# Reordering the passage from cross-attention to a quantised FFN in a one-core Trainium2 kernel

## The chip, the cores and the metric

The kernel runs on one core of one Trainium2 chip. The metric is the device time of one execution in microseconds (us). The engines are TensorE (PE in the profile, PEld for its weight loads), VectorE (DVE), ScalarE (ACT), GpSimd (POOL) and SyncE (SP), which issues most DMAs.

## The reference

x is 64 x 64 rows of 128, the context 64 x 64 rows of 256, all fp32. The first half is masked cross-attention with 8 heads of 16 and a residual, the second a feed-forward block whose three products take inputs quantised to FP4 in blocks of 16:

```python
src = (ctx @ W_src.T + b_src) * mask          # keys, values
q   = (layernorm(x) @ W_tgt.T + b_tgt) * mask
attn = softmax(where(mask == 0, -inf, q k / 4))
x = x + concat(layernorm(x), attn @ v) @ W_out.T + b_out
def fp4_quant_dequant(x):                     # blocks of 16
    scale = max(max(abs(block)) / 6, 1e-12)
    q = grid[searchsorted(mid, abs(x / scale))] * sign(x) * scale
xq = fp4_quant_dequant(layernorm(x))
h = silu(xq @ wq_gate.T) * (xq @ wq_up.T)     # 352 wide
out = x + fp4_quant_dequant(h) @ wq_down.T
```

## The kernel before, in words

The 4096 rows are 32 tiles of 128, in NG = 8 groups of 4 tiles (0 to 7). Every engine has its own program, written out by hand; semaphores are the only tie between them, and each engine works strictly in its written order. That order is what the change edits.

**Attention.** `attn_step(k)` runs for k = 0 to 8. In one step each engine works on several groups: key, query and value projections of group k, scores and softmax of k-1, attention product, out-projection and layer norm of k-2 and k-3, and quantisation of the FFN's input of k-3 and k-4. On TensorE a step goes scores (L954), attend (L988), spread_reciprocals (L1002), transposes of the normalised x, keys (L1017), two minus_max products, queries (L1025), two more minus_max, then `prob_transpose(g2, 0)` (L982), half of the values (`v_project`, L1030), `prob_transpose` 1 and 2, the other half, the last transposes and out_project (L1039). The values need the masked q (VectorE, `q_masked`, L694), since both use the PSUM bank w0. ScalarE does exponentials (L508), copies of the transposed probabilities (`probT_evac`, L516) and of keys and values. The context comes in four buffers cT, filled on SyncE's queue (L202).

**Quantising a group's FFN input** is a chain over three engines: VectorE adds the residual (`x2_add`, L729) and takes statistics (`stats2`, L690); POOL makes the scale (`rstd2_of`, L267) and the normalised rows (`xn2_of`, L274); VectorE takes block maxima (`block_max`, L735); POOL the scales (`scales2_of`, L286); VectorE their reciprocals (`block_reciprocal`, L742); POOL y (`y_of`, L306); ScalarE its magnitude (`y2_abs`, L521); VectorE rounds in two operations (`s3_round`, L747, L750 and L754); POOL multiplies back (`xq_of`, L313). The weights go the same way once; POOL's last product over all of them is L375, in step 3.

**FFN.** 16 units of two tiles. For tile m TensorE forms gate and up (`gate_up`, L1078; three PSUM banks in turn), ScalarE the silu (L537), VectorE the product (`h_product`, L838). For each unit VectorE takes maxima and reciprocals (L847, L854), ScalarE scales them (`h_inverse`, L617), POOL multiplies (`y_unit`, L386; its scales `h_scales`, L395), ScalarE takes the magnitude (`h_abs`, L598), VectorE rounds (`h_round`, L859, L864 and L869), POOL multiplies back (`hq_unit`, L401). Seven tiles later TensorE transposes h (L1096), ScalarE copies it, and TensorE multiplies with w_down (L1109). The quantisation of groups 5, 6 and 7 is written in between the units of these loops, at tiles `m` and units `u` given by numbers such as

```python
if m == 8:
    y2_abs(NG - 2)      # ScalarE, L646: group 6
if m == 9:
    s3_round(NG - 2)    # VectorE, L934
if u == 2:
    y_of(NG - 2)        # POOL, L454
```

## Time and profile before

| | |
|---|---|
| median of 3 runs | 204.89 us (204.83 to 205.24) |
| the profiled execution | 205.46 us |
| its span, first to last instruction | 203.2 us |
| busy: TensorE, VectorE, POOL, ScalarE | 185.8, 174.8, 141.2, 132.1 us |
| granted TensorE clock, mean | 0.995 |
| attention steps 0 to 7, with the start of scores in each from step 1 | 12.8, 25.3, 38.7, 51.2, 65.7, 78.5, 91.4, 103.9 us |
| first gate product, last store | about 113.4, the span's end |

The span is the time axis of all views; start times count from its beginning. A timeline row gives start, length, engine, line, output and input, and in brackets the idle time of that engine ahead of it with what ended it. A row with x4 stands for four instructions from the first start to the last end. Lengths of TensorE rows reach into the next row, since matmuls are pipelined: what one costs is the distance to the next start.

### The profile page before, as it was taken

The page shows a single profiled execution, that of the slowest core. Times are in us where ns is not written, and L with a number is a line of the kernel's source. Part 1 is how long each engine was busy: PE and PEld are TensorE (multiplying, and loading weights), DVE is VectorE, ACT ScalarE, POOL GpSimd, SP SyncE. Part 2 cuts the span into 40 slices and gives each one's busy share as a digit, 9 for nine tenths or more (in the row PEclk, how much of TensorE's full clock was granted, in tenths as well). Part 3 has the DMA queues.
Part 4 walks back from the last instruction along what each step waited for, and adds up shares of the span by engine and source line. Part 5 has one row for each costly group of instructions (what it writes and reads, how often), then busy time and mean ns, then how long its engine had stood idle before and what let it go on. Part 6 is the DMA issues. An engine that isn't in the chain of part 4 may idle for free.

```text
span 203.2 us, 5834 instructions
## 1 busy us (share of the span) xinstructions
PE 185.8 (91%) x2105; PEld 142.6 (70%) x2105; DVE 174.8 (86%) x383; ACT 132.1 (65%) x280; POOL 141.2 (70%) x206
## 2 busy tenths in 40 slices
PE   5889989999889999999998999689999998999881
PEld 5564866859649788596785775467878676877780
DVE  6558989988998988969868888999999999999861
ACT  2066997959778699696868735485566564656740
POOL 6353691678898685954919577797999966868870
PEclk9999999999999999999999999999999999999997
DMA  5799970401200000000000000000101100110013
GB/s 199 236 239 345 353 250 7 155 5 31 75 3 2 3 3 5 0 0 3 5 3 0 3 2 0 0 5 0 53 0 55 43 9 0 55 50 5 0 59 99
DMA packets 13698, 11.99 MB, mean 59 GB/s; under 512 B 790, under 2 KB 10590, under 8 KB 13670
## 3 DMA queue, kind: packets, MB, share of 16 engines
q1 hardware_dynamic: 13086, 11.23, 18.0%
q10 hardware_dynamic: 584, 0.39, 0.6%
q8 instruction: 17, 0.28, 0.5%
q14 instruction: 11, 0.09, 0.2%
HBM read 9.52 MB, written 2.10 MB: 57 GB/s over the span
## 4 chain that ended last, share of the span: by engine, by line
PE 50%; POOL 18%; issue 12%; DVE 8%; DMA 4%; ACT 4%; SPq 1%; POOLq 0%; ACTq 0%; DVEq 0%
PE bank L1034 7%; PE bank L1125 5%; PE bank L1022 5%; POOL wq_y L391 5%; DMA x_all<-in_x 4%; POOL xn L282 3%; POOL hq L406 3%; PE bank L1093 3%; PE bank L1090 3%; PE bank L985 3%; PE bank L1105 3%; PE bank L1028 3%; PE bank L997 3%; PE bank L971 2%; PE bank L1043 2%
## 5 line engine op out<-in xcount | busy, mean ns | idle before, releaser
L1125 PE MATMUL bank<-wdT,hT 128*128 128x128 f32 x186 | 26.4, 278 | 1.8 <-issue 0.8
L1090 PE MATMUL bank<-guT,xqT 128*128 128x352 f32 x64 | 24.6, 465 | 2.2 <-DVE hh L843 2.2
L1125 PEld LDWEIGHTS bank<-wdT,hT 128*128 128x128 f32 x186 | 23.2, 191 | 3.1 <-issue 1.9
L1093 PE MATMUL bank<-guT,xqT 128*128 128x352 f32 x64 | 24.2, 460 | 0.0
L406 POOL TENSOR_TENSOR hq<-wq_u,sch 128x704 f32<-128x704 f32 x15 | 21.2, 1411 | 3.6 <-DVE wq_u L869 3.5
L391 POOL TENSOR_TENSOR wq_y<-hh,ivh 128x704 f32<-128x704 f32 x15 | 21.1, 1407 | 3.4 <-ACT ivh L620 2.8
L715 DVE TENSOR_REDUCE den<-prob 128x8 f32<-128x512 f32 x32 | 19.8, 667 | 0.0
L614 ACT COPY hT<-bank 128x384 f32<-128x384 f32 x32 | 15.2, 474 | 5.1 <-PE bank L1105 5.1
L1034 PE MATMUL bank<-wsT,cT 128*128 128x128 f32 x128 | 17.6, 281 | 0.8 <-DVE q_m L700 0.8
L843 DVE TENSOR_TENSOR hh<-bank,mask_bc 128x352 f32<-128x352 f32 x32 | 15.9, 496 | 1.6 <-PE bank L1093 1.2
L1034 PEld LDWEIGHTS bank<-wsT,cT 128*128 128x128 f32 x128 | 15.4, 191 | 2.5 <-DVE q_m L700 2.3
L1105 PE MATMUL bank<-ident,hq 128*128 128x128 f32 x96 | 15.8, 274 | 1.5 <-POOL hq L406 0.9
L1105 PEld LDWEIGHTS bank<-ident,hq 128*128 128x128 f32 x96 | 12.0, 141 | 7.4 <-issue 3.0
L1093 PEld LDWEIGHTS bank<-guT,xqT 128*128 128x128 f32 x64 | 12.0, 190 | 7.0 <-ACT mask_bc L540 0.6
L504 ACT ACTIVATE k_bd<-bank,bk_of,head_of 128x512 f32<-128x512 f32 x16 | 12.5, 786 | 6.3 <-PE bank L1022 6.3
L540 ACT ACTIVATE mask_bc<-bank 128x352 f32<-128x352 f32 x32 | 14.7, 458 | 2.9 <-PE bank L1090 2.6
L1022 PE MATMUL bank<-cT,wsT 128*128 128x512 f32 x32 | 15.4, 600 | 0.7 <-issue 0.7
L601 ACT ACTIVATE a_pair<-wq_y 128x704 f32<-128x704 f32 x15 | 11.5, 766 | 6.8 <-DVE wq_u L869 5.3
L851 DVE TENSOR_REDUCE amh<-hh 128x44 f32<-128x748 f32 x16 | 14.9, 929 | 0.4
L670 DVE BATCH_NORM_STATS2 st<-x_all 128x6 f32<-128x128 f32 x64 | 13.6, 276 | 1.7 <-DMA x_all<-in_x 1.4
L282 POOL TENSOR_SCALAR xn<-x_all,nm,rs 128x128 f32<-128x128 f32 x32 | 14.4, 462 | 0.8
L869 DVE SCALAR_TENSOR_TENSOR wq_u<-a_pair,mask_bc 128x704 f32<-128x704 f32 x15 | 13.4, 892 | 0.5
(136 smaller groups left out, 503.8 us busy)
## 6 DMA issues: line engine op xcount, KB each, us to landing
cT<-in_ctxT SPq DMA_DIRECT2D x8, 512.0 KB, 5.2
x_all<-in_x SPq DMA_DIRECT2D x8, 256.0 KB, 6.7
mask_bc<-in_mask_rows SPq DMA_DIRECT2D x8, 256.0 KB, 6.7
out_y<-mask_bc SPq DMA_DIRECT2D x7, 256.0 KB, 2.2
wsT<-in_WsT ACTq DMA_DIRECT2D x1, 256.0 KB, 5.0
out_y<-mask_bc SPq DMA_DIRECT2D x1, 192.0 KB, 2.0
w_all<-in_wg SPq DMA_DIRECT2D x1, 176.0 KB
w_all<-in_wu SPq DMA_DIRECT2D x1, 176.0 KB
```

The source lines that it names most:

```text
L282: last = nc.gpsimd.tensor_scalar(xn2[:, j * NB_X:(j + 1) * NB_X, :].rearrange("p n k -> p (n k)"), x_all[:, n, :], nm2[:, n:n + 1], rs2[:, ...
L391: nc.gpsimd.tensor_tensor(yh[i][:, :, :], hh[i][:, :, 0:BLK], ivh[i][:, :].unsqueeze(2).to_broadcast([P, 2 * NB_H, BLK]), ALU.mult).then_i ...
L406: nc.gpsimd.tensor_tensor(hq[i][:, :, 0:I].rearrange("p t (n k) -> p t n k", k=BLK), rh[i][:, :, :].rearrange("p (t n) k -> p t n k", t=2) ...
L614: nc.scalar.copy(hT[n % 2][:, :, :].rearrange("p c t -> p (c t)"), t_bank[place % 2][:, 0:IP]).then_inc(t_ok, 1)
L715: nc.vector.tensor_reduce(den[:, :, p, :], prob[g % 2][p][:, :, :].rearrange("r j (e s) -> r j e s", e=2), AX.X, ALU.add).then_inc(sum_ok, 1)
L843: nc.vector.tensor_tensor(hh[u % 2][:, t * NB_H:(t + 1) * NB_H, 0:BLK], gu_bank[(2 * n + 1) % 3][:, 0:I].rearrange("p (n k) -> p n k", k=BLK),
L1022: last = nc.tensor.matmul(w1[:, :], wsT[:, c, 0:D], cT[g % 4][:, c, :], start=(c == 0), stop=(c == 1))
L1034: last = nc.tensor.matmul(w0[:, j * P:(j + 1) * P], cT[g % 4][:, c, j * P:(j + 1) * P], wsT[:, c, D:2 * D], start=(c == 0), stop=(c == 1))
L1090: nc.tensor.matmul(gu_bank[2 * n % 3][:, 0:I], xqT[g % 2][:, t], guT[:, 0, :], start=True, stop=True).then_inc(pe_g, 1)
L1093: nc.tensor.matmul(gu_bank[(2 * n + 1) % 3][:, 0:I], xqT[g % 2][:, t], guT[:, 1, :], start=True, stop=True).then_inc(pe_u, 1)
L1105: last = nc.tensor.transpose(t_bank[place % 2][:, c * P:(c + 1) * P], hq[u % 2][:, n % 2, c * P:(c + 1) * P], ident[:, :])
L1125: last = nc.tensor.matmul(bank[:, j * P:(j + 1) * P], hT[n % 2][:, c, :], wdT[:, c, :], start=(c == 0), stop=(c == 2))
```

## The change

- TensorE, every step: the second pair's `prob_transpose` stands ahead of the first half of the values.
- POOL, step 3: the product over the weights in four pieces; the weights' transposes wait for all four.
- Six context buffers in place of four; loads from the seventh on wait (L201 counts from 6). The two xqT buffers lie in the fifth, the two hT buffers in the sixth.
- Step 8, the passage: TensorE forms gate and up of tile 0 ahead of the transposes of the probabilities and gate 1 ahead of the out-projection; attend 7, its reciprocals, the transposes of group 1 and out-projection 7 follow later. ScalarE does all four exponentials, loads the silu table and does silu 0 and 1 among the copies of the transposed probabilities. VectorE takes the product of tile 0 ahead of the residual of group 6.
- The quantisation of groups 5 and 6 and the update and residual of group 7 move to later tiles on VectorE, ScalarE and POOL.

```diff
-        cT = [sb(f"cT{s}", [P, 2, GT]) for s in range(4)]
+        cT = [sb(f"cT{s}", [P, 2, GT]) for s in range(NG - 2)]
...
-        xqT = [sb(f"xqT{s}", [P, GT]) for s in range(2)]
+        xqT = [cT[NG - 4][:, s, :] for s in range(2)]
...
-        hT = [sb(f"hT{i}", [P, 3, P]) for i in range(2)]
+        hT = [cT[NG - 3][:, i, 0:IP].rearrange("p (c t) -> p c t", t=P) for i in range(2)]
...
-                sp.dma_start(cT[g % 4][:, :, :], cT_halves[:, :, g * GT:(g + 1) * GT]).then_inc(ld_c[g], 16)
+                past(sp, pe_v, g - NG + 3)
+                sp.dma_start(cT[g % (NG - 2)][:, :, :], cT_halves[:, :, g * GT:(g + 1) * GT]).then_inc(ld_c[g], 16)
...
-                    nc.gpsimd.tensor_tensor(w_all[:, :, :], wq_u[:, :, :],
-                                            wq_nsc[:, :].unsqueeze(2).to_broadcast([P, WALL, BLK]),
-                                            ALU.mult).then_inc(wq_ok, 1)
+                    for b in range(0, WALL, WALL // 4):
+                        w = slice(b, b + WALL // 4)
+                        nc.gpsimd.tensor_tensor(w_all[:, w, :], wq_u[:, w, :],
+                                                wq_nsc[:, w].unsqueeze(2).to_broadcast([P, WALL // 4, BLK]),
+                                                ALU.mult).then_inc(wq_ok, 1)
...
                 attn_step(k)
-            rstd2_of(NG - 2)
-            xn2_of(NG - 2)
 
...
                     hq_unit(u - 2)
-                if u == 5:
+                if u == 6:
                     xq_of(NG - 2)
                 if u < UNITS:
                     h_scales(u)
@@ -449,8 +449,11 @@
                 if u == 0:
                     xq_of(NG - 3)
                 if u == 1:
+                    rstd2_of(NG - 2)
+                    xn2_of(NG - 2)
+                if u == 2:
                     scales2_of(NG - 2)
-                if u == 2:
+                if u == 3:
                     y_of(NG - 2)
                 if u == 5:
                     rstd2_of(NG - 1)
...
-                if on(g2):
+                if k == NG:
+                    for p in range(PAIRS):
+                        exp(g2, p)
+                    nc.scalar.activation(warm[:, :], minus_half[:, :], ACT.Silu)
+                    silu(0)
+                    probT_evac(g2, 0)
+                    probT_evac(g2, 1)
+                    silu(1)
+                    probT_evac(g2, 2)
+                elif on(g2):
                     exp(g2, 0)
                     exp(g2, 1)
                     exp(g2, 2)
                     probT_evac(g2, 0)
                     exp(g2, 3)
-                    if k == NG:
-                        nc.scalar.activation(warm[:, :], minus_half[:, :], ACT.Silu)
                     probT_evac(g2, 1)
                     probT_evac(g2, 2)
                 if on(g1) and k > 0:
...
+                if 2 <= m < NT:
                     silu(m)
+                if m == 2:
+                    y2_abs(NG - 3)
+                    av_evac(NG - 1)
                 if m % 2 == 0 and 0 < m < NT:
                     h_inverse(m // 2 - 1)
-                if m == 0:
-                    av_evac(NG - 1)
-                if m % TILES == 1 and on(m // TILES + 1):
+                if m == 2:
+                    xqT_evac(1)
+                if m % TILES == 1 and m > 1 and on(m // TILES + 1):
                     xqT_evac(m // TILES + 1)
-                if m == 0:
-                    y2_abs(NG - 3)
-                if m == 8:
+                if m == 9:
                     y2_abs(NG - 2)
...
                     weights_round_down()
-                if k == NG:
-                    x2_add(NG - 2)
-                    stats2(NG - 2)
-                if on(g4) and g4 < NG - 3:
+                if on(g4):
                     s3_round(g4)
-
-            for k in range(NG + 1):
-                attn_step(k)
 
...
-            for m in range(NT + LAG + 2):
+            for k in range(NG):
+                attn_step(k)
+            x2_add(NG - 3)
+            stats2(NG - 3)
+            for p in range(PAIRS):
+                row_max(NG - 1, p)
+            update(NG - 2)
+            row_sum(NG - 1, 0)
+            block_max(NG - 3)
+            for p in range(1, PAIRS):
+                row_sum(NG - 1, p)
+            h_product(0)
+            reciprocals(NG - 1)
+            block_reciprocal(NG - 3)
+            x2_add(NG - 2)
+
+            for m in range(1, NT + LAG + 2):
...
-                if m == 0:
+                if m == 2:
                     s3_round(NG - 3)
+                if m == 10:
+                    s3_round(NG - 2)
                 if m % 2 == 0 and 0 <= m // 2 - 2 < LAST_U:
                     h_round(m // 2 - 2)
                 if m == 2 * LAST_U + 4:
@@ -922,16 +945,16 @@
                 if m % 2 and m < NT:
                     h_max(m // 2)
                     h_reciprocal(m // 2)
-                if m == 0:
+                if m == 3:
                     update(NG - 1)
-                if m == 3:
+                if m == 4:
+                    stats2(NG - 2)
+                if m == 5:
                     x2_add(NG - 1)
-                if m == 4:
+                if m == 6:
                     block_max(NG - 2)
-                if m == 6:
+                if m == 8:
                     block_reciprocal(NG - 2)
-                if m == 9:
-                    s3_round(NG - 2)
...
                     minus_max(g2, 3)
+                    if k == NG:
+                        gate(0)
+                        up(0)
                     prob_transpose(g2, 0)
+                    prob_transpose(g2, 1)
                 if on(g1) and k > 0:
                     v_project(g1, 0)
                 if on(g2):
-                    prob_transpose(g2, 1)
                     prob_transpose(g2, 2)
                 if k == 1:
                     prob_transpose(0, 3)
@@ -1179,6 +1207,8 @@
                     bias_of_values()
                 elif on(g2):
                     prob_transpose(g2, 3)
+                if k == NG:
+                    gate(1)
                 if on(g3):
                     out_project(g3)
                 if 0 <= k - 4 < 3:
@@ -1186,14 +1216,16 @@
 
             for k in range(NG + 1):
                 attn_step(k)
-            gate_up(0)
-            attend(NG - 1)
-            for m in range(NT + LAG + 1):
-                if 1 <= m < NT:
-                    gate_up(m)
-                if m == 1:
+            up(1)
+            for m in range(2, NT + LAG + 1):
+                if m < NT:
+                    gate(m)
+                    up(m)
+                if m == 2:
+                    attend(NG - 1)
                     spread_reciprocals(NG - 1)
-                if m == 2:
+                    xq_transpose(1)
+                if m == 4:
                     out_project(NG - 1)
                 if m % TILES == 1 and on(m // TILES + 1):
                     xq_transpose(m // TILES + 1)
```

Three places show what this does to the order on an engine. The lines of the changed kernel differ a little from those before (L521's Abs is L527's row, L838's product L848, L690's statistics L681 and L686).

VectorE at the end of the attention and in the first tiles, before. x_all is the residual of group 6, BN_STATS and BN_AGGR its statistics, hh the product of tile 0, u and r the rounding of group 5, updT the update of group 7:

```order
L721 RECIPROCAL rden<-den 128x32
L733 TENSOR_TENSOR x_all<-bank,x_all 128x512
L670 BN_STATS st<-x_all 128x6 x4
L675 BN_AGGR mv<-st 128x2 x4
L843 TENSOR_TENSOR hh<-bank,mask_bc 128x22x16
L750 SCALAR_TENSOR_TENSOR u<-a,y 128x512
L754 SCALAR_TENSOR_TENSOR r<-a,u 128x512
L727 TENSOR_TENSOR updT<-bank,updU 128x512
L843 TENSOR_TENSOR hh<-bank,mask_bc 128x22x16
```

VectorE with the change, from the product of tile 3 (the first row; amh and ivr are maximum and reciprocal of unit 1, the two SCALAR_TENSOR_TENSOR rows the rounding of unit 0):

```order
L848 TENSOR_TENSOR hh<-bank,mask_bc 128x22x16
L856 TENSOR_REDUCE amh<-hh 128x44
L862 RECIPROCAL ivr<-amh 128x44
L738 TENSOR_TENSOR updT<-bank,updU 128x512
L848 TENSOR_TENSOR hh<-bank,mask_bc 128x22x16
L869 SCALAR_TENSOR_TENSOR mask_bc<-a_pair,wq_y 128x704
L874 SCALAR_TENSOR_TENSOR wq_u<-a_pair,mask_bc 128x704
L681 BN_STATS st<-x_all 128x6 x4
L686 BN_AGGR mv<-st 128x2 x4
L848 TENSOR_TENSOR hh<-bank,mask_bc 128x22x16
```

The statistics of group 6 stood ahead of tile 0 and now stand behind tile 4 and the rounding of unit 0.

POOL before, from the scales of group 6 (up, sc); hq and sch belong to the units, wq_y is a unit's y, the row y<-xn,iv is y of group 6:

```order
L289 TENSOR_SCALAR up<-am 128x32
L291 TENSOR_SCALAR sc<-am 128x32
L406 TENSOR_TENSOR hq<-wq_u,sch 128x2x352
L398 TENSOR_SCALAR sch<-amh 128x44
L391 TENSOR_TENSOR wq_y<-hh,ivh 128x704
L309 TENSOR_TENSOR y<-xn,iv 128x512
L406 TENSOR_TENSOR hq<-wq_u,sch 128x2x352
```

POOL with the change, from the normalised rows of group 6 (xn), which stand just ahead of the first hq:

```order
L282 TENSOR_SCALAR xn<-x_all,nm,rs 128x128 x4
L406 TENSOR_TENSOR hq<-wq_u,sch 128x2x352
L398 TENSOR_SCALAR sch<-amh 128x44
L391 TENSOR_TENSOR wq_y<-hh,ivh 128x704
L289 TENSOR_SCALAR up<-am 128x32
L291 TENSOR_SCALAR sc<-am 128x32
L406 TENSOR_TENSOR hq<-wq_u,sch 128x2x352
L398 TENSOR_SCALAR sch<-amh 128x44
L391 TENSOR_TENSOR wq_y<-hh,ivh 128x704
L309 TENSOR_TENSOR y<-xn,iv 128x512
```

Scale and normalised rows of group 6, which stood ahead of the first unit, stand behind y of unit 1, and y of group 6 has moved from ahead of the second hq to behind y of unit 3.

ScalarE before, from the inverse of unit 3 (ivh); mask_bc rows are silus (9 and 10 here), a<-y is the Abs of group 6, hT and xqT rows are copies of transposes, a_pair the Abs of unit 3:

```order
L620 ACTIVATE ivh<-ivr 128x44
L524 ACTIVATE a<-y 128x512
L614 COPY hT<-bank 128x384
L540 ACTIVATE mask_bc<-bank 128x352
L608 COPY xqT<-bank 128x512
L614 COPY hT<-bank 128x384
L601 ACTIVATE a_pair<-wq_y 128x2x352
L540 ACTIVATE mask_bc<-bank 128x352
```

ScalarE with the change; the first row is silu 9, the last but one silu 10, the cT rows are the xqT and hT copies:

```order
L543 ACTIVATE mask_bc<-bank 128x352
L618 COPY cT<-bank 128x512
L527 ACTIVATE a<-y 128x512
L624 COPY cT<-bank 128x384
L611 ACTIVATE a_pair<-wq_y 128x2x352
L543 ACTIVATE mask_bc<-bank 128x352
L630 ACTIVATE ivh<-ivr 128x44
```

The Abs of group 6 moves from ahead of silu 9 to ahead of silu 10, behind the copy of group 3's transposes.

## Rows read from the trace of the kernel before

**Rows 1.** Busy time by stretch, core 0: window, length, busy of each engine
```profile
150.00:170.00 20.00, 18.77 (x110) 14.14 (x108) 19.21 (x30) 11.11 (x27) 15.66 (x20) 1.00 0.09 27
170.00:189.00 19.00, 18.91 (x115) 14.93 (x116) 18.35 (x30) 11.84 (x28) 14.96 (x15) 1.00 0.10 29
```

**Rows 2.** Timeline of TensorE, step 5: start, us, line, tiles, idle before
```profile
72.56 0.60 PE L985 MATMUL bank<-ident,prob 128*128 128x128 f32 x4
73.14 1.16 PE L1034 MATMUL bank<-wsT,cT 128*128 128x128 f32 x8
74.13 0.60 PE L985 MATMUL bank<-ident,prob 128*128 128x128 f32 x4
74.57 0.60 PE L985 MATMUL a_pair<-ident,prob 128*128 128x128 f32 x4
```

**Rows 3.** Timelines of POOL, of VectorE and of TensorE, steps 3 and 4
```profile
49.70 2.59 POOL L375 TENSOR_TENSOR w_all<-wq_u,wq_nsc 128x1408 f32<-128x1408 f32 x1
...
52.98 0.64 POOL L260 TENSOR_SCALAR nm<-mv 128x4 f32<-128x4 f32 x1
...
55.58 0.20 POOL L269 TENSOR_SCALAR ve<-mv 128x4 f32<-128x4 f32 x1 [0.69 <-DVE mv L675]
...
50.71 2.13 DVE L750 SCALAR_TENSOR_TENSOR u<-a,y 128x512 f32<-128x512 f32 x1 [0.50 <-ACT a L524]
...
58.90 0.60 PE L985 MATMUL bank<-ident,prob 128*128 128x128 f32 x4
60.31 1.16 PE L1034 MATMUL bank<-wsT,cT 128*128 128x128 f32 x8 [0.81 <-DVE q_m L700]
```

**Rows 4.** Timeline of POOL, last unit: the product in two halves
```profile
190.71 1.52 POOL L417 TENSOR_TENSOR wq_y<-hh,ivh 128x352 f32<-128x352 f32 x2 [0.36 <-ACT ivh L620]
```

**Rows 5.** Timeline of TensorE, passage
```profile
109.35 1.04 PE L985 MATMUL bank<-ident,prob 128*128 128x128 f32 x8
...
111.62 0.39 PE L1043 MATMUL bank<-woT,xnT 128*128 128x128 f32 x2
...
113.41 0.76 PE L1090 MATMUL bank<-guT,xqT 128*128 128x352 f32 x2
...
114.69 1.10 PE L997 MATMUL bank<-probT,val 128*32 128x64 f32 x64
```

**Rows 6.** Timeline of VectorE, passage
```profile
114.62 0.87 DVE L670 BATCH_NORM_STATS2 st<-x_all 128x6 f32<-128x128 f32 x4
...
115.82 0.49 DVE L843 TENSOR_TENSOR hh<-bank,mask_bc 128x352 f32<-128x352 f32 x1
```

**Rows 7.** Timeline of VectorE, FFN
```profile
134.11 0.88 DVE L864 SCALAR_TENSOR_TENSOR mask_bc<-a_pair,wq_y 128x704 f32<-128x704 f32 x1
...
137.69 0.63 DVE L750 SCALAR_TENSOR_TENSOR u<-a,y 128x512 f32<-128x512 f32 x1
...
139.40 0.88 DVE L864 SCALAR_TENSOR_TENSOR mask_bc<-a_pair,wq_y 128x704 f32<-128x704 f32 x1
...
165.61 1.76 DVE L754 SCALAR_TENSOR_TENSOR r<-a,u 128x512 f32<-128x512 f32 x1
```

**Rows 8.** Timeline of POOL, passage and first units
```profile
116.00 0.20 POOL L269 TENSOR_SCALAR ve<-mv 128x4 f32<-128x4 f32 x1 [1.28 <-DVE mv L675]
...
117.56 2.16 POOL L282 TENSOR_SCALAR xn<-x_all,nm,rs 128x128 f32<-128x128 f32 x4
...
127.88 0.32 POOL L289 TENSOR_SCALAR up<-am 128x32 f32<-128x32 f32 x1 [1.64 <-DVE am L739]
...
132.09 1.06 POOL L309 TENSOR_TENSOR y<-xn,iv 128x512 f32<-128x512 f32 x1
...
135.01 1.39 POOL L391 TENSOR_TENSOR wq_y<-hh,ivh 128x704 f32<-128x704 f32 x1
```

**Rows 9.** Timeline of ScalarE around the Abs of group 7
```profile
160.66 0.63 ACT L524 ACTIVATE a<-y 128x512 f32<-128x512 f32 x1 [1.96 <-POOL y L309]
...
162.25 0.46 ACT L540 ACTIVATE mask_bc<-bank 128x352 f32<-128x352 f32 x1
```

More of the change, by code:

```diff
@@ L1021, in k_project @@
                 for c in range(2):
-                    last = nc.tensor.matmul(w1[:, :], wsT[:, c, 0:D], cT[g % 4][:, c, :], start=(c == 0), stop=(c == 1))
+                    last = nc.tensor.matmul(w1[:, :], wsT[:, c, 0:D], cT[g % (NG - 2)][:, c, :], start=(c == 0), stop=(c == 1))
                 last.then_inc(pe_k, 1)
```

13 lines of the change are left out of this document (6 added, 7 removed).

## The prediction

> **What bounds the kernel now.** I read three views: the busy time by stretch, to see which engine has no slack where; the timeline of each engine, with the idle time ahead of each row; and the waits, to see who ends them. The attention steps follow each other at what TensorE needs, about 12.8 us, with one small hole in each. Behind the passage VectorE sets the pace: from 150 to 170 us it is busy 19.21 of 20 us, TensorE 18.77, and only from 170 us on TensorE is full, 18.91 of 19 us, against 18.35 of VectorE [rows 1]. So a microsecond won before 115 us is kept only if VectorE and GpSimd (POOL) keep it through 115 to 165 us. Faster or slower by over 0.2% (0.41 us) is what a measurement of this kernel can tell from no change.
>
> **Second transposes in front of the values.** In step 5 the first pair's transposes start at 72.56 and the first value product at 73.14; four transposes need 0.44 (74.13 to 74.57), so TensorE stands for 0.14, waiting for VectorE's masked q [rows 2]. With the second pair's transposes in between, their exponentials being done by then, the hole is filled: 0.14 in each of six steps, 0.84 us. Step 4 has 0.81 to 0.97 us of idle there [rows 3] and is taken with the next edit.
>
> **POOL's weight product in four pieces.** The single product runs 2.59 us from 49.70. VectorE's first rounding of group 0 starts at 50.71 and takes 2.13 us where the same operation needs 0.63 at 137.69: it waited for the product's end [rows 3, 7]. Two products of half the usual length take 1.52 where one of the full length takes 1.39 [rows 4, 8], so a cut costs some 0.13 us, three cuts 0.4. VectorE gets in between pieces and gains up to 1.0 us. POOL does not: 2.59 + 0.4 + two roundings of 0.65 in between end it at 54.0, not 52.29. The four small operations behind it took 2.6 us (to 55.58 less 0.69 of waiting), held up by the roundings as the row at 52.98 shows, 0.64 for what takes 0.20 [rows 3, 8]; without that some 1.8. They now end at 55.8, so the scale of the second statistics starts 0.25 later than at 55.58, and masked q hangs on it. So POOL takes over from VectorE as the late one: step 4 gains between 0.44 - 0.25 = 0.19 (POOL decides) and 0.97 (all of the hole). I take 0.35, nearer the POOL end. [...]
>
> **Six context buffers.** Loads 6 and 7 start 10 to 25 us earlier on SyncE's queue and nothing is queued behind them but mask loads; no product waits for a context load after step 0. Zero. The input for the FFN and the transposed h lie in two of the six buffers, whose last readers are long done: zero.
>
> So the attention half brings **1.2 us** (bounds 1.0 and 1.8).
>
> **The passage**, in the times of the trace before, without these 1.2. TensorE has the minus-max products done at 109.35 [rows 5] and then does not stop: gate and up of tile 0 (113.41 to 114.69 with a gap, 1.2), sixteen transposes (1.76), gate 1 (0.59), out-projection 6 (113.41 - 111.62 = 1.79), up 1, gate and up 2 (1.8), attend 7 (1.1), its reciprocals and the transposes of group 1 (0.9), gate and up 3 (1.2): 10.3 us, to 119.7. Silu ahead of the copies lets VectorE form tile 0 some 3 us earlier than its 115.82 [rows 6], and tile 3 at 119.9. That is the gain, and it is paid for. The table load now stands in front of silu 0, with row sums of VectorE beside it: zero. The statistics of group 6, at 114.62 before [rows 6], stand in unit m=4, behind update 7 and the first rounding. From tile 3: product, maximum and reciprocal with one rounding pair 3.58 (134.11 to 137.69), update 7, a product, statistics 1.2 (114.62 to 115.82): 5.8 us, 125.7 (update and product: 0.6 and 0.4) [rows 6, 7]. POOL, idle since y of unit 1, starts group 6 there, not at 116.00 [rows 8]: 1.56 for the scale, some 1.75 for xn2 (its 2.16 in rows 8 met a rounding), hq 0, scales, y 2 and the group's scales 4.21 (127.88 to 132.09), hq 1 and scales 1.9 (132.09 to 135.01 less 1.0 of y), y 3 1.4: y of group 6 starts at 136.5 and ends at 137.4, where it began at 132.09 before.
>
> Now ScalarE. Its Abs of group 6 stands ahead of silu 10. Before, at the same place for group 7, it stood 1.96 us for POOL's y, and the silu behind it began 1.59 us after the Abs [rows 9]. Now: Abs at 137.5, silu 10 at 139.1, product 10 at 139.6. VectorE is through with reciprocal 4 at 137.7 and stands 1.9 us. Even with POOL free this does not go away: y of group 6 needs the block reciprocal that VectorE makes just before product 9 (135.8), so 1.06 of y, 1.59 and 0.46 stand against 1.86 of VectorE's work, 1.3 us of idle.
>
> Then the roundings of group 6. POOL's y of unit 4 and VectorE's first rounding both follow silu 10, y by some 0.15 us sooner. It runs 1.39 us, and VectorE waits as it did at 50.71 and at 165.61, where 1.76 stands for some 0.7 [rows 3, 7]: some 1.2 us. Were VectorE first, its second rounding would meet the delayed y: the same price. So the rounding of unit 3 starts at 139.6 + 1.71 (roundings and a product, 137.69 to 139.40) + 1.2 = 142.5, where it started at 139.40 [rows 7]: **3.1 us late**. From there to 162 us VectorE had no idle before, so nothing gives it back. POOL, with xq of group 6 moved from unit 5 to 6 and 3 us of waiting for unit 3, reaches y of group 7 another 0.5 later, which the same ScalarE wait passes on; I take 0.2 of it. Bounds of the passage: -0.8 (the lead on VectorE kept, no stall) and +3.65.
>
> **Sum.** -1.2 + 3.1 + 0.2 = +2.1 us. The profiled execution took 205.46 (span 203.2 and 2.26 around it), which gives 207.56; it lies 0.57 above the median 204.89, so 207.0.
>
> **Rivals.**
> (1) Faster: the lead carries. If POOL has y of group 6 ready before ScalarE comes to it at some 135.3, neither the stall nor the meeting on the roundings happens, and VectorE keeps 0.8 us of its lead: -1.2 - 0.8 = -2.0, 202.9. It decides at 2 us less on POOL between the statistics and that y. For it: before, group 6 had some 3 us to spare there, and VectorE starts the FFN some 3 us earlier. Against it: the reciprocal's own place in the order.
> (2) The stall without the meeting on the roundings: 1.9 + 0.2 - 1.2 = +0.9, 205.8. Two events 0.15 us apart are hardly settled by my adding. The Trainium skill (SBUF — State Buffer, Who interferes with whom) has it that the one of VectorE with two SBUF inputs and a POOL reader that issues second blocks fully, and that issue order decides. By that rule the price is the rest of whichever is running: that is what rows 3 and 7 show.
> (3) The fill does nothing: the loop from Abs over statistics, POOL and masked q back to the Abs was as long as TensorE's step before. It loses 0.44 by the fill, so I hold it for slack; if q is still late, only 0.2 is won: +3.1, 208.0.
> (4) The pieces cancel: gains near 1.8 and a stall of 1.3 with half a meeting, within 0.2% of before.
>
> **How the numbers follow.** Forecast 0.42 (own range 206.1 to 207.9), rival 1 0.28, rival 2 0.16, rival 3 0.05, rival 4 0.09. Faster is rival 1: 0.28. Within 0.2%: 0.09. Slower: the rest, 0.63. The range takes in most of rival 1 and the upper bound but for its tail: 202.6 to 208.0.
>
> **What would show it.** Right: steps of 12.7 us in the attention with no hole at the first values; VectorE's first h maximum 3 to 5 us earlier; POOL idle some 2 us before group 6's scale; ScalarE's second Abs of the FFN waiting for POOL 1.5 us or more; VectorE idle over 1 us ahead of product 10 and a rounding of over 1.5 us there. Wrong: that Abs not waiting, or VectorE's idle there under 0.5 us; then rival 1 or 4 holds. Step 4 shorter by over 0.8 us would say that POOL was not the next late one.

## The result, and the profile after

The changed kernel takes 206.44 us (median of 8 runs, 205.70 to 207.03) against 205.00 (8 runs) of the kernel before on the same chip: ratio 1.0063, 95% interval 1.0045 to 1.0080, **slower by 1.3 us** (1.4 by the medians). The forecast was 207.0, slower by 2.1. Its profiled execution took 206.55, span 204.7.

| | before | after |
|---|---|---|
| scores of group 0 start at | 12.79 | 12.92 |
| scores of groups 1, 2, 3, 4, 7 start at | 25.32, 38.72, 51.24, 65.69, 103.89 | 25.16, 39.11, 51.39, 65.61, 103.08 |
| VectorE's rounding of unit 3 | 139.40 | 141.71 |
| VectorE's product 20 | 162.73 | 165.83 |
| TensorE's last product | 197.74 | 200.85 |
| end of the span | 203.2 | 204.7 |

Scores of group g run in step g + 1, so the eight starts in the table of the kernel before are those of steps 1 to 8, and what the expectations below call "the scores of step 7" (103.89) are group 7's, in step 8. Step 2 lasts from the scores of group 1 to those of group 2.

Read downward, the table says three things. The attention half won 0.81 us (0.94 counted from the first scores). The passage made of it 3.1 of lateness by product 20, which TensorE carried to its last product. And the very end gave 1.6 of it back.

Busy time by stretch. The columns are window and length, busy time of TensorE, its weight loads, VectorE, ScalarE and POOL with the number of instructions, then granted clock, busy share of the DMA engines and GB/s. First one stretch of the kernel before, then the changed kernel; its last two lines answer to [rows 1]:

```profile
115.00:150.00 35.00, 32.23 (x227) 23.41 (x217) 32.36 (x65) 19.46 (x44) 27.92 (x34) 1.00 0.03 9
```

```profile
100.00:115.00 15.00, 14.38 (x215) 11.72 (x214) 12.14 (x29) 11.18 (x22) 7.91 (x14) 1.00 0.01 3
115.00:150.00 35.00, 28.38 (x206) 20.56 (x205) 30.94 (x61) 17.04 (x38) 24.45 (x31) 0.95 0.03 9
150.00:170.00 20.00, 20.00 (x122) 15.71 (x121) 18.70 (x29) 12.85 (x29) 17.84 (x21) 1.00 0.09 27
170.00:189.00 19.00, 18.18 (x106) 13.79 (x106) 18.37 (x29) 10.96 (x25) 13.45 (x13) 1.00 0.10 29
```

From 115 to 150 us TensorE is busy 28.4 of 35 us, where it was 32.2, and its granted clock there is 0.95: that stretch is where the time goes.

**Attention.** TensorE in step 5, against [rows 2]: all eight transposes together, and the values behind them without a hole.

```profile
72.47 1.04 PE L1008 MATMUL bank<-ident,prob 128*128 128x128 f32 x8
73.34 1.06 PE L1057 MATMUL bank<-wsT,cT 128*128 128x128 f32 x8
74.24 0.60 PE L1008 MATMUL a_pair<-ident,prob 128*128 128x128 f32 x4
```

The product in pieces, against [rows 3]: POOL, VectorE's two roundings, POOL's scale, VectorE's block maxima and masked q, and TensorE's first values of step 4.

```profile
50.09 3.92 POOL L377 TENSOR_TENSOR w_all<-wq_u,wq_nsc 128x352 f32<-128x352 f32 x4
...
50.86 1.31 DVE L761 SCALAR_TENSOR_TENSOR u<-a,y 128x512 f32<-128x512 f32 x1 [0.26 <-ACT a L527]
52.20 1.16 DVE L765 SCALAR_TENSOR_TENSOR r<-a,u 128x512 f32<-128x512 f32 x1
...
55.93 0.20 POOL L269 TENSOR_SCALAR ve<-mv 128x4 f32<-128x4 f32 x1
...
59.26 0.69 DVE L750 TENSOR_REDUCE am<-xn 128x32 f32<-128x512 f32 x1 [1.00 <-POOL xn L282]
59.86 0.74 DVE L711 SCALAR_TENSOR_TENSOR q_m<-bank,b_kvq,mask_bc 128x512 f32<-128x512 f32 x1
60.66 1.16 PE L1057 MATMUL bank<-wsT,cT 128*128 128x128 f32 x8 [0.84 <-DVE q_m L711]
```

The pieces end at 54.01, predicted 54.0; that they agree so well is luck, for they start 0.39 later than at 49.70 and take 3.92, not the 4.3 of the prediction. POOL's scale has lost its wait of 0.69 and still starts 0.35 later than at 55.58, of which 0.15 is the lateness of group 3's scores; VectorE now stands 1.00 for POOL. POOL is the late one, as predicted, and the values still wait for masked q.

**A stop that was not in the sum.** Between the two halves of one key projection, where no wait stands, TensorE stops in step 2. First the kernel before, then the changed one (the second half's row):

```profile
30.49 1.02 PE L1022 MATMUL bank<-cT,wsT 128*128 128x512 f32 x2 [0.72 <-issue]
```

```profile
31.12 1.02 PE L1045 MATMUL bank<-cT,wsT 128*128 128x512 f32 x2 [1.51 <-issue]
```

**Passage.** The changed kernel's VectorE, POOL, ScalarE and TensorE, with most rows between these left out:

```profile
115.27 0.93 DVE L856 TENSOR_REDUCE amh<-hh 128x44 f32<-128x748 f32 x1
123.70 0.86 DVE L681 BATCH_NORM_STATS2 st<-x_all 128x6 f32<-128x128 f32 x4
...
125.06 0.20 POOL L269 TENSOR_SCALAR ve<-mv 128x4 f32<-128x4 f32 x1 [2.23 <-DVE mv L686]
135.79 1.06 POOL L309 TENSOR_TENSOR y<-xn,iv 128x512 f32<-128x512 f32 x1
136.88 0.63 ACT L527 ACTIVATE a<-y 128x512 f32<-128x512 f32 x1 [2.10 <-POOL y L309]
138.47 0.46 ACT L543 ACTIVATE mask_bc<-bank 128x352 f32<-128x352 f32 x1
138.96 0.53 DVE L848 TENSOR_TENSOR hh<-bank,mask_bc 128x352 f32<-128x352 f32 x1 [1.79 <-ACT mask_bc L543]
139.13 1.38 POOL L391 TENSOR_TENSOR wq_y<-hh,ivh 128x704 f32<-128x704 f32 x1 [0.50 <-ACT ivh L630]
139.40 1.67 DVE L761 SCALAR_TENSOR_TENSOR u<-a,y 128x512 f32<-128x512 f32 x1
141.71 0.88 DVE L869 SCALAR_TENSOR_TENSOR mask_bc<-a_pair,wq_y 128x704 f32<-128x704 f32 x1
143.60 1.39 POOL L406 TENSOR_TENSOR hq<-wq_u,sch 128x704 f32<-128x704 f32 x1 [3.08 <-DVE wq_u L874]
144.65 0.91 PE L1150 MATMUL bank<-wdT,cT 128*128 128x128 f32 x6 [2.08 <-issue]
146.24 1.38 PE L1118 MATMUL bank<-guT,cT 128*128 128x352 f32 x2
```

The Abs of group 6 is the row of L527, silu 10 the one of L543, product 10 the one of L848. This is the forecast's chain link by link: VectorE's first maximum 4.35 us earlier than at 119.62; POOL idle 2.23 ahead of group 6's scale; y of group 6 late; ScalarE's Abs waiting 2.10 (I had 2.2); VectorE idle 1.79 ahead of product 10 (1.9); and its first rounding of group 6, 1.67 us where [rows 7] has 0.63, beside POOL's y of unit 4. The Trainium skill (SBUF — State Buffer, Who interferes with whom), cited in the prediction, has it that the one that issues second is blocked fully. The trace agrees: y runs from 139.13 to 140.51, the rounding is issued second, at 139.40, and ends 0.56 behind y.

Two links more were not in it. TensorE stands 2.08 ahead of the down product at 144.65, the first of group 1. It waits for VectorE's residual of group 0 (143.87 to 144.55), which is queued behind those roundings; the profile's "issue" has no releaser for it, but the wait written ahead of line 1150 is for that residual. (The expectation of e12 calls it group 2's.) Then TensorE works slowly: gate and up take 1.38 for 0.76, and the granted clock from 145 to 150 us is 0.66, between its 1.2 and 2.4 GHz levels.

**The end.** TensorE's last product and the last two stores, before and after:

```profile
197.74 0.94 PE L1125 MATMUL a_pair<-wdT,hT 128*128 128x128 f32 x6
...
198.71 0.29 DVE L882 TENSOR_TENSOR mask_bc<-a_pair,x_all 128x128 f32<-128x128 f32 x1 [0.28 <-PE a_pair L1125]
...
out_y<-mask_bc SPq DMA_DIRECT2D x1, 64.0 KB, 3.8
```

```profile
200.85 0.94 PE L1150 MATMUL a_pair<-wdT,cT 128*128 128x128 f32 x6
201.48 0.56 DVE L887 TENSOR_TENSOR mask_bc<-bank,x_all 128x384 f32<-128x384 f32 x1 [2.44 <-DMA out_y<-mask_bc]
...
out_y<-mask_bc SPq DMA_DIRECT2D x1, 64.0 KB, 1.7
```

The same last store landed in 3.8 us before and in 1.7 after. That is how 3.1 of lateness became 1.5 of span; why it landed sooner is open (see the end).

### The profile page after: what moved, and what is told of

Read it like the earlier page. It is cut to its first block, busy times and chain, and to the rows that moved or that the text cites. A ratio compares the mean times of both kernels' runs of the same rounds, so it can differ in the third digit from the quotient of the medians.

```text
span 204.7 us, 5837 instructions
## 1 busy us (share of the span) xinstructions
PE 185.0 (90%) x2105; PEld 143.5 (70%) x2105; DVE 175.9 (86%) x383; ACT 132.4 (65%) x280; POOL 142.3 (70%) x209
## 4 chain that ended last, share of the span: by engine, by line
PE 59%; POOL 15%; issue 10%; DVE 7%; DMA 5%; ACT 2%; SPq 1%; DVEq 0%; POOLq 0%; ACTq 0%
PE bank L1057 6%; PE bank L1150 5%; PE bank L1118 5%; PE bank L1045 5%; PE bank L1112 5%; DMA x_all<-in_x 4%; PE bank L1020 4%; PE bank L1066 3%; PE bank L1067 3%; PE a_pair L1008 3%; PE bank L994 3%; PE bank L1051 3%; PE bank L1008 3%; POOL wq_y L391 3%; PE bank L1130 2%
## 5 line engine op out<-in xcount | busy, mean ns | idle before, releaser
L1150 PE MATMUL bank<-wdT,cT 128*128 128x128 f32 x186 | 26.5, 278 | 4.4 <-issue 2.9
L1150 PEld LDWEIGHTS bank<-wdT,cT 128*128 128x128 f32 x186 | 23.4, 193 | 5.7 <-issue 3.6
L1112 PE MATMUL bank<-guT,cT 128*128 128x352 f32 x64 | 24.6, 466 | 0.5 <-DVE hh L848 0.5
L1118 PE MATMUL bank<-guT,cT 128*128 128x352 f32 x64 | 24.9, 472 | 0.0
L624 ACT COPY cT<-bank 128x384 f32<-128x384 f32 x32 | 15.2, 474 | 8.0 <-PE bank L1130 7.8
L543 ACT ACTIVATE mask_bc<-bank 128x352 f32<-128x352 f32 x32 | 14.7, 460 | 7.8 <-PE bank L1112 7.0
L848 DVE TENSOR_TENSOR hh<-bank,mask_bc 128x352 f32<-128x352 f32 x32 | 16.1, 504 | 3.9 <-ACT mask_bc L543 2.9
L1057 PE MATMUL bank<-wsT,cT 128*128 128x128 f32 x128 | 16.9, 277 | 0.8 <-DVE q_m L711 0.8
L1118 PEld LDWEIGHTS bank<-guT,cT 128*128 128x128 f32 x64 | 12.2, 194 | 7.1 <-ACT mask_bc L543 0.8
L681 DVE BATCH_NORM_STATS2 st<-x_all 128x6 f32<-128x128 f32 x64 | 13.6, 275 | 1.8 <-DMA x_all<-in_x 1.6
L282 POOL TENSOR_SCALAR xn<-x_all,nm,rs 128x128 f32<-128x128 f32 x32 | 13.9, 448 | 0.8
```

The source lines that it names most:

```text
L624: nc.scalar.copy(hT[n % 2][:, :, :].rearrange("p c t -> p (c t)"), t_bank[place % 2][:, 0:IP]).then_inc(t_ok, 1)
L848: nc.vector.tensor_tensor(hh[u % 2][:, t * NB_H:(t + 1) * NB_H, 0:BLK], gu_bank[(2 * n + 1) % 3][:, 0:I].rearrange("p (n k) -> p n k", k=BLK),
L1057: last = nc.tensor.matmul(w0[:, j * P:(j + 1) * P], cT[g % (NG - 2)][:, c, j * P:(j + 1) * P], wsT[:, c, D:2 * D], start=(c == 0), stop=(c ...
L1112: nc.tensor.matmul(gu_bank[2 * n % 3][:, 0:I], xqT[g % 2][:, t], guT[:, 0, :], start=True, stop=True).then_inc(pe_g, 1)
L1118: nc.tensor.matmul(gu_bank[(2 * n + 1) % 3][:, 0:I], xqT[g % 2][:, t], guT[:, 1, :], start=True, stop=True).then_inc(pe_u, 1)
L1150: last = nc.tensor.matmul(bank[:, j * P:(j + 1) * P], hT[n % 2][:, c, :], wdT[:, c, :], start=(c == 0), stop=(c == 2))
```

## Experiments

Ratios are against the kernel before, on the same chip in the same hours, with 95% intervals. Since they are good to some 0.3% (0.6 us), the finer statements rest on places in the traces. Two things blur even those. The scores of group 0 start at 12.66 to 13.75 us, and not by the edits: e1 has 13.54 where e10 with the same edit has 12.66, and two executions of one program differ too (12.79 before, 12.66 in e9). The last column takes that out. And the kernel before was itself not equally fast beside all of them: 205.28 beside e1 to e4, 204.04 beside e5 to e8, 205.07 beside e9 to e12, 205.00 beside the changed kernel, which was not timed beside e5 to e8. So their ratios may stand up to 0.5% too high when they are held against its 1.0063.

| kernel | ratio | interval | TensorE's last product | group 0's scores | between the two |
|---|---|---|---|---|---|
| before | 1 |  | 197.74 | 12.79 | 184.95 |
| changed kernel | 1.0063 | 1.0045 to 1.0080 | 200.85 | 12.92 | 187.93 |
| e1_fill | 0.9920 | 0.9894 to 0.9947 | 196.79 | 13.54 | 183.25 |
| e2_pieces | 0.9996 | 0.9969 to 1.0023 | 197.91 | 12.66 | 185.25 |
| e3_buffers | 1.0037 | 1.0007 to 1.0068 | 199.77 | 13.75 | 186.02 |
| e4_attention | 0.9921 | 0.9888 to 0.9954 | 197.31 | 12.95 | 184.36 |
| e5_passage | 1.0179 | 1.0149 to 1.0208 | 201.49 | 12.66 | 188.83 |
| e6_late_loads | 1.0065 | 1.0032 to 1.0098 | 199.91 | 12.66 | 187.25 |
| e7_abs_later | 1.0010 | 0.9984 to 1.0036 | 199.45 | 12.66 | 186.79 |
| e8_stats_earlier | 1.0176 | 1.0139 to 1.0213 | 202.66 | 12.74 | 189.92 |
| e9_before_again | 0.9976 | 0.9948 to 1.0005 | 197.56 | 12.66 | 184.90 |
| e10_fill_pieces | 0.9883 | 0.9847 to 0.9920 | 195.84 | 12.66 | 183.18 |
| e11_later_and_late | 0.9805 | 0.9762 to 0.9847 | 194.64 | 12.66 | 181.98 |
| e12_unit_first | 1.0038 | 1.0015 to 1.0062 | 201.21 | 13.13 | 188.08 |

### The attention half in parts: e1, e2, e3, e4

e1 moves one line of the kernel before:

```
                     prob_transpose(g2, 0)
+                    prob_transpose(g2, 1)
...
-                    prob_transpose(g2, 1)
                     prob_transpose(g2, 2)
```

> The kernel before with one edit: the second pair's transposes in front of the first values, in all steps. In the changed kernel the score products of step 7 came 0.81 us earlier than before; step by step the lead was +0.16, -0.39, -0.15, +0.08, +0.33, +0.57, +0.81, so each step from the third on gained some 0.24 and the second lost 0.55, where TensorE stood 1.51 us inside the key projection, against 0.72 before. Theory (the early context loads cause that longer stop): without them this kernel keeps 0.72 there and gains 0.24 in each of six steps, 1.4 at the scores of step 7. It should lie 1.4 below the kernel before unless the passage swallows it: 203.6. Rival (the stop belongs to the new order of the instructions, wherever the loads are): 1.5 us of stop here too, gain 0.8, 204.2. My prediction's own price of the fill was 0.84.

e2 has only the product of line 377 in four pieces, with the wait of the weight transposes at 4.

> The kernel before with one edit: POOL's weight product in four pieces. Theory (POOL takes over from VectorE as the late one): VectorE's first rounding of group 0 takes about 1.3 in place of 2.13, POOL's scale of the second statistics starts within 0.4 of 55.58, masked q of that step comes 0 to 0.35 later than at 59.51, and the whole is the same as before, 205.0 within 0.3. Rival (the hole in step 4 closes): the 0.81 ahead of the values at 60.31 shrinks below 0.4, and the whole is 204.5.

e3 has only the six buffers and the loads' new wait:

```
-                past(sp, pe_v, g - 3)
+                past(sp, pe_v, g - NG + 3)
```

> The kernel before with one edit: six context buffers, two of them lent later to the FFN's input and the transposed h, so that the last three context loads and two mask loads start by 25 us. Theory (early loads hold up TensorE's instructions): the stop inside the key projection at 30 us grows from 0.72 to about 1.5, and the whole is 0.8 slower, 205.8, or less if VectorE had slack. Rival: 0.72 stays and so does the time, 205.0 within 0.3.

e4 has all three.

> All three edits of the attention half with the passage of before. The lead at the scores of step 7 should be the 0.81 of the changed kernel, in both theories. If the passage of before keeps it, 204.2; if VectorE or POOL in the passage swallow it, 204.6 to 205.0. The passage edits then cost the rest of the distance to 206.4.

The fill alone gives 0.8%, 1.6 us. From the scores of group 1 to those of group 7, steps 2 to 7, the kernel before needs 78.57 us and e1 77.15: **1.42** for the fill, some 0.24 a step (0.19 in step 4). Step 1 gains by it as well: it takes 12.54 in e2, e5 and e9 and 12.24 in e1 and e10, 0.30 less, which makes 1.72 in seven steps. The pieces alone change nothing (0.9996); their 0.06 is the difference between e1 and e10 (77.09). In e2 VectorE's first rounding takes 1.07 for 2.13, but POOL's scale starts at 55.73 and masked q at 59.66: the theory of e2 holds, POOL takes over.

The buffers alone cost. Step 2, from scores to scores: 13.40 (before), 13.73 (e2), 13.37 (e5) and 13.40 (e9) with late loads and no fill, 14.47 in e3; with the fill 13.14 (e1), 13.23 (e6), 13.14 (e10), 13.22 (e11) with late loads, and 13.95 (after), 14.32 (e4), 13.97 (e7), 14.05 (e8), 14.04 (e12) with early ones: **0.9 to 1.0 us**, and no early one overlaps a late one. It sits in the stop between the two halves of the key projection. It is the loads' time and not the six buffers, which e6 and e11 keep. (The trace of e3 is of an execution of 207.41 us, above its median of 206.24; its step 2 fits the other early ones.) The theory of e3 holds: the stop is 1.79, and the kernel 0.8 us slower. Rows of that second half in e3, e4 and e6:

```profile
32.52 1.02 PE L1022 MATMUL bank<-cT,wsT 128*128 128x512 f32 x2 [1.79 <-issue]
```

```profile
31.51 1.02 PE L1024 MATMUL bank<-cT,wsT 128*128 128x512 f32 x2 [1.88 <-issue]
```

```profile
30.14 1.02 PE L1045 MATMUL bank<-cT,wsT 128*128 128x512 f32 x2 [0.79 <-issue]
```

What the loads do there, before and after (last two columns: busy share of the DMA engines, GB/s):

```profile
25.00:33.00 8.00, 6.96 (x150) 4.44 (x151) 7.25 (x18) 7.06 (x16) 5.86 (x8) 1.00 0.56 181
```

```profile
25.00:33.00 8.00, 6.33 (x148) 4.21 (x149) 7.47 (x17) 6.28 (x15) 6.55 (x8) 1.00 0.91 334
```

The trace shows one thing more that comes over the DMA engines. A queue of its own carries the instructions; in the changed kernel's list of queues (packets, MB, share of 16 engines):

```profile
q8 instruction: 17, 0.28, 0.5%
```

These are 17 packets of 16 KB, most of them some 1 us long. The queue must be TensorE's: it runs over 4200 instructions, the next engine some 600. The second packet is the one at this place: it starts at 28.83 in the changed kernel and at 27.93 before. In all 14 traces the second half of the key projection starts 1.28 to 1.54 us after the end of that packet, though the stop ahead of it goes from 0.3 (e1, e10) to 1.88 (e4). And the packet starts 2.1 to 2.9 us after the scores of group 1 with late loads, and 3.6 to 4.0 with early ones. So what TensorE waits for here is its own instructions, and the early loads, which keep the DMA engines 0.91 busy instead of 0.56, put their packet off by about a microsecond. This is read from the constant distance; no run changes the fetch alone, and what in the DMA engines puts the packet off is not shown.

The Trainium skill (Runtime: NRT & Kernel Launch, Instruction fetch mechanics) has it that an engine's sequencer fetches its instructions in blocks over a DMA queue of its own, mostly hidden. The trace agrees on blocks and queue; hidden the fetch was not at this place.

So the rival for e1 falls, with a stop of 0.3 there where it asked for 1.5. And e4 wins no more than e1 (0.9921 and 0.9920); counted from the first scores its last product comes 1.18 behind e10's. Its lead at group 7's scores is 0.43, or 0.59 so counted, less than the 0.81 expected.

### The two halves apart: e5, e6

e5 has the new passage and the old attention half.

> The passage of the changed kernel with the attention half of before (transposes, product, buffers and loads as before). If the two halves add up, the passage costs what lies between the attention half alone (0.9921 of before) and the whole change (1.0063): 1.4 per cent, 2.9 us, so 207.9 against 205.0. My prediction's price was 3.1 + 0.2 = 3.3: 208.3. Rival (the passage is dear only because the attention half ahead of it runs early or sits in other buffers): below 206.4. In the profile: ScalarE's Abs of group 6 waits about 2 us for POOL's y, VectorE idle 1.8 ahead of product 10, rounding of unit 3 about 3.1 after 139.40.

e6 is the changed kernel with the old wait in front of the context loads.

> The changed kernel with one edit: context loads 5 to 7 wait as in the kernel before, six buffers kept. Theory (loads that run beside step 2 hold up TensorE's instructions): TensorE's stop inside the key projection at 30 us falls from 1.51 to between 0 and 1.04, the scores of step 7 come at 102.0 to 102.6 in place of 103.08, and the whole is 0.5 to 1.0 faster than 206.4: 205.7. Rival (the stop is there with late loads too, or VectorE's lateness in the passage hides it): 206.4 within 0.3.

e5 is 1.8% slower, 3.7 us: the halves add up (0.9921 and 1.0179 make 1.010, good to some 0.4%, which overlaps the 1.0045 to 1.0080 of the whole; in the last column -0.59 and +3.88 make 3.29, against 2.98). Its Abs and the product behind it:

```profile
137.54 0.63 ACT L525 ACTIVATE a<-y 128x512 f32<-128x512 f32 x1 [2.09 <-POOL y L309]
...
139.62 0.53 DVE L846 TENSOR_TENSOR hh<-bank,mask_bc 128x352 f32<-128x352 f32 x1 [1.79 <-ACT mask_bc L541]
```

Measured from its scores of group 7 (103.74 against 103.89), unit 5's reciprocal, behind the roundings, comes 3.1 late (146.08 against 143.11) and product 20 3.9 late (166.48 against 162.73): the passage costs 3.1 as worked out, and 0.8 more by product 20, where I had 0.2. It does this with the clock at 1.00 throughout, and product 20 comes 62.74 us behind group 7's scores, in the changed kernel 62.75: so the slow TensorE there added nothing. There VectorE waited 0.39 ahead of product 20, here 1.21: what the clock cost, ScalarE's second Abs would have cost anyway.

e6 won 0.98 at the scores of group 7 (102.10; 0.72 counted from the first scores) and 0.94 at the last product (199.91). The ratio does not show it: 1.0065, with an interval that reaches 1.0032. By the medians it is 205.30 against 206.44, but beside a kernel before that ran 1 us faster too; so the times leave e6 open.

### The passage: e7, e8, e12

```
-                if m == 9:
+                if m == 11:
                     y2_abs(NG - 2)
...
-                if m == 10:
+                if m == 12:
                     s3_round(NG - 2)
```

> The changed kernel with one edit: ScalarE's Abs of group 6 from m=9 to m=11 and VectorE's roundings of group 6 from m=10 to m=12. Theory (the wait for POOL's y stands on the path): the Abs waits for nothing, silu 10 starts right after silu 9, VectorE's idle of 1.79 ahead of product 10 is gone, rounding of unit 3 starts 1.8 to 3 us earlier than at 141.71, and the whole is 1.8 to 3.0 faster: 204.0. Rival (the wait only stands where VectorE has slack later, or another takes its place because the roundings of group 6 and 4 fall together): above 205.6.

e7 is faster than the changed kernel, by 0.5% in the ratios (1.0010 against 1.0063) and by 1.14 us from the first scores to the last product: the wait was on the path. ScalarE's Abs and VectorE's first rounding of group 6:

```profile
139.74 0.62 ACT L527 ACTIVATE a<-y 128x512 f32<-128x512 f32 x1
...
144.42 0.82 DVE L761 SCALAR_TENSOR_TENSOR u<-a,y 128x512 f32<-128x512 f32 x1
```

Neither waits, and unit 3's rounding starts at 138.28, 3.4 earlier. The gain is 1.1 us and not the 1.8 to 3.0 expected. In this execution TensorE's clock fell, to 0.66 from 130 to 135 us, and VectorE then waited 0.67 and 0.41 for it. That is not the rule for e7: its 12 executions show a mean clock of 0.992 in four (median 205.07 us) and of 0.999 or 1.000 in eight (203.70). So where the clock falls it costs e7 1.4 us, and the traced execution is one of the four; without the fall its 1.1 would be some 2.5, an estimate, and within what was expected. The next waits remained: 2.62 of ScalarE for y of group 7, 1.22 of VectorE ahead of product 20, and a second rounding of group 7 of 1.76.

In e8 the statistics of group 6 stand straight behind the residual sum of group 6.

> The changed kernel with one edit: VectorE's statistics of group 6 from m=4 to straight behind the first residual sum of the passage, as in the kernel before. Theory A (POOL's late start makes the stall): POOL starts the scale near 116 in place of 125.06, y of group 6 waits for nothing when ScalarE comes, the whole is 2 to 3 faster, 204.0. Theory B (my prediction: the block reciprocal, which VectorE makes just ahead of product 9, holds y back also with POOL free): the Abs still waits 1.0 to 1.6, the whole is 0.3 to 1.2 faster, 205.6.

Both theories fell: e8 is 1.1% slower than the changed kernel.

```profile
118.82 1.76 DVE L765 SCALAR_TENSOR_TENSOR r<-a,u 128x512 f32<-128x512 f32 x1
...
123.04 0.49 PE L1065 MATMUL bank<-woT,xnT 128*128 128x128 f32 x2 [2.91 <-DVE updT L738]
...
124.26 0.20 POOL L269 TENSOR_SCALAR ve<-mv 128x4 f32<-128x4 f32 x1
```

POOL starts group 6 at 124.26, not near 116: on its own queue that scale stands behind y of unit 1. What came forward on VectorE was no use to POOL, and pushed everything else back: a rounding of group 5 met POOL's y of unit 0 (1.76 for 0.7), update 7 came later, and out-projection 7 on TensorE waited 2.91 for it in place of 1.48. The Abs still waited 2.05.

e12 turns the order at m=10:

```
                 if m % 2 == 0 and 0 <= m // 2 - 2 < LAST_U:
                     h_round(m // 2 - 2)
+                if m == 10:
+                    s3_round(NG - 2)
```

> The changed kernel with one edit: at m=10 VectorE rounds unit 3 first and group 6 behind it. Theory (the meeting of VectorE's first rounding of group 6, 1.67 us, with POOL's y of unit 4 delays unit 3, and through it POOL's hq, the residual of group 2 and TensorE's down product that waits for it): unit 3's rounding starts at 139.4 in place of 141.71, its two operations take 0.9 each, POOL's hq starts near 141.2 in place of 143.60, TensorE's stop of 2.08 ahead of the down product falls below 1.2 or moves, the clock stays at its full level, and the whole is 0.3 to 1.2 faster: 205.6. Rival (VectorE has the same work up to that residual, so nothing but hq comes earlier): 206.4 within 0.3.

```profile
139.69 0.88 DVE L869 SCALAR_TENSOR_TENSOR mask_bc<-a_pair,wq_y 128x704 f32<-128x704 f32 x1
...
141.57 1.76 POOL L406 TENSOR_TENSOR hq<-wq_u,sch 128x704 f32<-128x704 f32 x1 [0.76 <-DVE wq_u L874]
142.13 1.76 DVE L765 SCALAR_TENSOR_TENSOR r<-a,u 128x512 f32<-128x512 f32 x1
...
145.02 0.91 PE L1150 MATMUL bank<-wdT,cT 128*128 128x128 f32 x6 [2.16 <-issue]
```

Unit 3 does start 2.0 us earlier, its operations take 0.9, and beside POOL's y the rounding of a pair with one input in PSUM is not slowed. But now POOL's hq starts earlier and meets group 6's roundings: hq 1.76 for 1.39, second rounding 1.76 for 0.69. The residual ends no sooner, and TensorE stops 2.16. The rival holds: the meeting costs the same in either order (1.0038 against 1.0063, overlapping intervals; 188.08 against 187.93 in the last column). In this trace TensorE's clock stayed at full level behind the same stop. That says nothing of the edit: in 8 of its 12 executions e12 shows a mean clock of 0.990 to 0.992, as the changed kernel does in 6 of 8, and they take no longer than the others.

### What beats both: e9, e10, e11

e9 is the kernel before, for its trace.

> The kernel before, unchanged, for its trace. From TensorE's last product to the end of the program its trace showed 5.46 us (197.74 to 203.2), the changed kernel's 3.85 (200.85 to 204.7), and so of 3.11 us of lateness 1.5 were left. If that belongs to the old passage, 5.1 to 5.5 again, as in the five other kernels that have it; if it is chance, anything from 3.3. The stop inside the key projection should lie between 0.2 and 1.1, as in the kernels whose loads are late.

Chance, then: last product at 197.56 and the span's end at 201.1, 3.5 us, where the first trace had 5.46. The stop in the key projection is 0.35, within what was expected. Its ratio of 0.9976 also shows how well two equal programs agree.

> The kernel before with the second pair's transposes ahead of the values and POOL's product in four pieces, loads and passage as before: the attention half without what cost it 1.05 us. Adding up: the fill gave 0.24 in each of six steps, the pieces 0.05, the buffers are left out, so 1.5 below the kernel before, 203.5 to 203.9 against 205.3, or 0.993; scores of step 7 at 102.1 to 102.5. If the early loads' 1.05 us is real, this is also 1.0 below the attention half with them, 0.9921 minus 0.5 per cent: 0.987. The two expectations differ by what the passage of before lets through.

e10, fill and pieces only, is 1.2% faster than the kernel before, near the 0.987 expected if the loads' cost is real, with the scores of group 7 at 101.99, 1.80 ahead of e9's 103.79. The passage of before lets the lead through whole: last product 195.84 against 197.56 in e9, 1.7 us.

e11 is the changed kernel with the loads as before, e7's edit, and for group 7:

```
-                if m == 19:
+                if m == 20:
                     y2_abs(NG - 1)
...
-                if m == 20:
+                if m == 21:
                     s3_round(NG - 1)
```

> The changed kernel with three edits: loads as before, Abs and roundings of group 6 two units of m later, those of group 7 one later (Abs m=20, roundings m=21). With group 6 alone ScalarE's Abs of group 7 waited 2.62 us for POOL's y and VectorE stood 1.22 ahead of product 20. Theory (these waits are the passage's cost): neither Abs waits over 1 us, VectorE stands under 0.5 ahead of product 20, and the whole is 0.9 (loads) + 0.8 less than 1.001 of before: 0.993. Rival (the FFN is held by VectorE's and TensorE's own work from 150 us on): 0.998 or more.

It is the fastest of all: 201.59 us against 205.07, 0.9805 of before, **3.5 us** by the medians and 4 by the ratio, more than expected. Its Abs of groups 6 and 7 and VectorE's roundings of group 7:

```profile
137.35 0.62 ACT L527 ACTIVATE a<-y 128x512 f32<-128x512 f32 x1
...
161.03 0.61 ACT L527 ACTIVATE a<-y 128x512 f32<-128x512 f32 x1
...
164.72 0.63 DVE L761 SCALAR_TENSOR_TENSOR u<-a,y 128x512 f32<-128x512 f32 x1
165.39 0.69 DVE L765 SCALAR_TENSOR_TENSOR r<-a,u 128x512 f32<-128x512 f32 x1
```

No wait on either Abs, none on product 20, no meeting with POOL. From the reciprocal of unit 9 to that of unit 11 it needs 9.72 us (160.42 to 170.14), e10 with the old places 11.38 (159.96 to 171.34): 1.66 is what group 7's Abs cost in the kernel before as well, 0.44 of waiting ahead of product 20 and 1.07 of meeting (the 1.76 of [rows 7] for 0.69) among it. Against e7 the last product comes 4.8 earlier: 0.8 from the loads, 1.6 between the reciprocals of units 3 and 5, where e7's clock had fallen and e11's had not, and 2.4 between those of units 9 and 11 (12.15 in e7).

## Why the prediction was right, and where it was not

**Sign and mechanism** hold. The forecast's passage came to 3.1 at the rounding of unit 3. e5 measures 3.1 there, with ScalarE's wait and VectorE's idle 0.11 shorter each than worked out. That the sum is good to 0.1 is in part luck: product 10 comes 0.2 later than in the sum, and the meeting costs 1.04 (2.75 from product 10 to unit 3's rounding, less 1.71) and not 1.2. e7 takes wait and meeting away and gets back 1.1 in a trace with a fallen clock, some 2.5 without it.

**The attention half** was -1.2 in the sum and -0.81 in the trace, or -0.94 from the first scores. Three terms are behind it. The fill was mis-sized: 0.84 for six steps, 0.14 each, taken from the idle in [rows 2]. It measures 1.53 in those six and 0.19 in step 4. A step wins the hole of 0.14 and 0.09 more, because the first value product, started behind a wait, took 0.99 (73.14 to 74.13 [rows 2]) and takes 0.90 without one (73.34 to 74.24); step 1 wins 0.30. Step 4 gained 0.23 by fill and pieces where I took 0.35, at the POOL end of its bounds, and e2 shows 0.06 for the pieces. The step that failed is "**Six context buffers** ... Zero": I looked for who waits for the loads, and none does; I did not ask what the loads share. They cost 0.9 to 1.0, by putting off TensorE's instructions. Two errors of opposite sign, 0.6 of gain and 0.9 of cost left out, made the half look nearly right.

**Behind the passage** 0.2 stood for POOL's later y of group 7; it was 0.8. VectorE's idle ahead of product 20 rose from 0.44 to 1.21 (e5), which is most of it.

**The sum** in the trace is thus +3.1, not +2.1, up to the last product. The end gave 1.6 back by the last store, which nothing in my sum could have. The right range owes something to that.

**Rivals.** (1) needed POOL to have y ready for the Abs; it does not in after, e5, e6 or e8. Moving the Abs instead of POOL's work makes the same come true: e11. Its chance of 0.28 was too high for the change as made, since my own reading of the reciprocal's place spoke against it. (2) falls, the meeting is in the trace; its 205.8 is about as near to 206.44 (0.6) as my 207.0 is (0.6), so the time alone does not tell them apart. (3) falls by e1. (4) falls by e5.

## What to carry to other kernels

When work is brought forward, look at the queue of every engine in its chain: here an Abs in ScalarE's queue, one place too early for POOL, turned a lead of 4 us into a lag of 3. With that Abs two tiles later, group 7's one tile later and the loads late again, the changed kernel went from 1.0063 to 0.9805. Statistics brought forward on one engine are of no use if the next engine's own order has them later (e8). And early loads are not free because nobody waits for them: ask what else comes over the same DMA engines, the engines' own instructions among it.
